# Gate's last products ahead of up's, a signal of silu's own, and an earlier turn of h in the last tiles of a mixture-of-experts layer

## The chip, the cores and the metric

The kernel runs on one core of one Trainium2 chip. The metric is the device time in microseconds. Where a time comes from a profile, it is counted from the start of the profiled span.

## What is computed

`x` has 4 x 512 tokens of 512 numbers. Each token goes through a linear layer with a low-rank adapter chosen per batch; the result `y` goes through a top-2 mixture of 16 experts, and the experts' weighted output is added to `x`. Cut to what matters here:

```python
def _L0_ffn_ref(hidden_states, gate_w, w_gate, w_up, w_down):
    ...
    g = jnp.einsum('th,eih->tei', x, w_gate)
    u = jnp.einsum('th,eih->tei', x, w_up)
    h = jax.nn.silu(g) * u
    expert_out = jnp.einsum('tei,ehi->teh', h, w_down)
    y = jnp.einsum('te,teh->th', combine, expert_out)
```

Hidden size is 512, an expert's inner size 352 (three parts of 128, 128 and 96), everything in float32.

## The kernel before

A first phase computes `y`, the router and tables that sort the 4096 token-expert pairs by expert, in **tiles** of 128 pairs of one expert. There are at least 32 tiles (`NFULL`) and at most 47 (`NTILE`); the number is found on the chip, and with these inputs it is 40, tiles 0 to 39. From tile 32 on each engine's code stands in branches on that count.

Each engine has its own program, written in order, and semaphores join them. For a tile t:

- GpSimd gathers its 128 rows of `y` into `xg`, and later scatters the result `ys` into `out`, adding.
- TensorE transposes `xg` into bank 0 (`x_turn`, L569). ScalarE rounds it to `xt_hi` (L732), VectorE takes the rest as `xt_lo` (L1067). A float32 product is made of three: hi x hi, hi x lo, lo x hi, for which the weights too are split, once per expert, into `w_hi` (ScalarE, L340) and `w_lo` (VectorE, L342) from `w_raw`.
- `gate_up` (L636): for each quarter k of the 512 inner rows six products of 352 columns, three for gate into bank 2 or 3, three for up into bank 4 or 5, the two taken in turns. After the 24th `m_gu` is raised.
- ScalarE waits for `m_gu` and makes `sg` = silu(gate) (L779). VectorE waits for `a_sg` and multiplies it by up: `hh` (L1079). TensorE transposes `hh` into bank 1 (`h_turn`, three transposes, L613), ScalarE rounds that to `ht_hi` (L769), VectorE makes `ht_lo` (L1072, raises `v_ht`).
- `down` (L657): nine products of 512 columns into bank 6 or 7, three for each of three inner parts k. ScalarE scales the bank by the token's weight: `ys` (L788).

The order on TensorE is by hand. In iteration t of the main loop, up to 32, it is h_turn(t-1), x_turn(t+1), gate_up(t), down(t-1). From tile 32 on h_turn(t) stands inside down(t-1):

```python
if t + 1 >= NFULL and t + 1 < NTILE and k == KI - 1:
    h_turn(t + 1)
```

that is, after six of the nine products. VectorE's order in an iteration from 32 on is: ht_lo of the tile before (once, at 32), the gate_up part of tile t+1's `w_lo` if its expert is new, xt_lo(t+1), hh(t), ht_lo(t), the down part of `w_lo`. ScalarE's is xt_hi(t+1), the gate_up part of `w_hi` for tile t+2, silu(t), the down part for t+1, ht_hi(t), ys(t-1); at 32, ht_hi(31) stands ahead of these.

## Time and profile before

| | us |
|---|---|
| median of 3 runs | 366.63 |
| runs | 365.82, 366.63, 366.96 |
| the profiled execution's own time | 366.1 |
| its span, first to last instruction | 364.3 |
| TensorE busy | 349.9 (96%) |
| VectorE busy | 198.1 (54%) |
| ScalarE busy | 179.3 (49%) |

The mean granted TensorE clock is 0.993 of full speed. The page names L636 and L657, gate_up and down, for 36% and 20% of the chain that ended last. TensorE's matmuls are pipelined: the time of one (0.32 us for 352 columns) overlaps the next, so the rate is read from start to start. PE is TensorE, PEld its weight loads, which run ahead of the products; DVE is VectorE, ACT ScalarE, POOL GpSimd, SP SyncE; a q behind a name means its sequencer.

### The profile page before, as it was taken

To read this page: it belongs to the slowest core of one execution; us is meant where nothing else is said; L and a number is where in the kernel's file an instruction comes from. 1 tells how busy PE (TensorE), PEld (TensorE's weight loads), DVE (VectorE), ACT (ScalarE), POOL (GpSimd) and SP (SyncE) were. 2 spreads that over 40 slices of the span, in tenths; PEclk is the share of its full clock that TensorE was granted. 3 is DMA by queue.
4 is the path that set the end of the run, shared out by engine and by line. 5 is a ranking of instruction groups with operands and counts; after the bars stand their busy time and mean duration, and the time that the engine had idled before them with its cause. 6 is when DMAs were issued, how large, how long until landed. Compare 5 with 4: busy or idle time off the path is not lost.

```text
span 364.3 us, 7564 instructions
## 1 busy us (share of the span) xinstructions
PE 349.9 (96%) x2033; PEld 310.0 (85%) x2033; DVE 198.1 (54%) x274; ACT 179.3 (49%) x242; POOL 129.4 (36%) x85
## 2 busy tenths in 40 slices
PE   8999989999999999999999999999999999999980
PEld 4777778879989999999999999999999998898960
DVE  0566799894546355444665527556282656556210
ACT  2488611622575544445755466464545557554320
POOL 0000000042534354366644526546264554232131
PEclk9999999999999999999999999999999999999997
DMA  7994763766498758669598684976929295921322
GB/s 278 398 444 144 297 231 120 271 227 221 119 346 288 223 130 226 153 146 319 111 302 252 180 280 68 299 207 186 332 44 304 62 248 176 303 33 14 48 34 36
DMA packets 28913, 73.78 MB, mean 203 GB/s; under 512 B 3440, under 2 KB 3568, under 8 KB 28784
## 3 DMA queue, kind: packets, MB, share of 16 engines
q1 hardware_dynamic: 19904, 54.30, 42.4%
q0 software_dynamic: 8960, 18.89, 24.0%
q8 instruction: 23, 0.38, 0.4%
q14 instruction: 26, 0.21, 0.2%
HBM read 60.59 MB, written 19.92 MB: 221 GB/s over the span
## 4 chain that ended last, share of the span: by engine, by line
PE 81%; DMA 6%; issue 6%; DVE 2%; ACT 1%; DVEq 1%; POOLq 1%; SPq 0%; POOL 0%; ACTq 0%
PE bank L636 36%; PE bank L657 20%; PE bank L569 4%; PE bank L613 4%; PE bank L507 4%; PE bank L508 3%; PE bank L509 3%; PE bank L404 3%; DMA xg<-y_rows,gidx 2%; DMA w_raw<-wall 2%; DMA head_sb<-head 2%; PE bank L435 1%; PE bank L555 1%; PE bank L517 1%; DVE hh L1079 1%
## 5 line engine op out<-in xcount | busy, mean ns | idle before, releaser
L1152 POOL DMA_INDIRECT out<-ys,sidx x40 | 75.4, 1886 | 131.0 <-ACT ys L788 60.5
L342 DVE TENSOR_TENSOR w_lo<-w_raw,w_hi (+2 forms) x32 | 76.4, 2389 | 22.0 <-ACT w_hi L340 16.5
L1131 POOL DMA_INDIRECT xg<-y_rows,gidx x40 | 53.4, 1335 | 97.8 <-issue 83.4
L636 PE MATMUL bank<-w_hi,xt_hi 128*128 x320 | 80.8, 333 | 0.3 <-issue 0.3
L636 PE MATMUL bank<-w_hi,xt_lo 128*128 x320 | 77.2, 322 | 0.0
L636 PE MATMUL bank<-w_lo,xt_hi 128*128 x320 | 77.2, 322 | 0.0
L340 ACT ACTIVATE w_hi<-w_raw (+2 forms) x32 | 64.8, 2024 | 10.1 <-issue 6.1
L779 ACT ACTIVATE sg<-bank 128x352 f32<-128x352 f32 x40 | 18.6, 464 | 79.0 <-PE bank L636 75.9
L636 PEld LDWEIGHTS bank<-w_hi,xt_lo 128*128 128x128 f32 x320 | 55.8, 188 | 0.0
L636 PEld LDWEIGHTS bank<-w_lo,xt_hi 128*128 128x128 f32 x320 | 55.7, 188 | 0.0
L636 PEld LDWEIGHTS bank<-w_hi,xt_hi 128*128 128x128 f32 x320 | 53.9, 189 | 1.3 <-issue 1.3
L1079 DVE TENSOR_TENSOR hh<-sg,bank 128x352 f32<-128x352 f32 x40 | 20.7, 518 | 56.1 <-ACT sg L779 56.1
L657 PE MATMUL bank<-w_hi,ht_hi 128*128 (+1 forms) x120 | 47.9, 399 | 0.9 <-ACT ys L788 0.9
L1072 DVE TENSOR_TENSOR ht_lo<-bank,ht_hi 128x384 fp32r<-128x384 f32 x40 | 22.2, 555 | 48.5 <-ACT ht_hi L769 48.5
L657 PE MATMUL bank<-w_lo,ht_hi 128*128 (+1 forms) x120 | 47.2, 394 | 0.0
L657 PE MATMUL bank<-w_hi,ht_lo 128*128 (+1 forms) x120 | 47.0, 392 | 0.0
L788 ACT ACTIVATE ys<-bank,wtab 128x512 f32<-128x512 f32 x40 | 27.3, 683 | 32.7 <-PE bank L657 31.1
L1067 DVE TENSOR_TENSOR xt_lo<-bank,xt_hi 128x512 fp32r<-128x512 f32 x40 | 27.4, 686 | 3.5 <-ACT xt_hi L732 3.5
L657 PEld LDWEIGHTS bank<-w_hi,ht_lo 128*128 128x128 f32 (+1 forms) x120 | 22.5, 188 | 5.0
L657 PEld LDWEIGHTS bank<-w_hi,ht_hi 128*128 128x128 f32 (+1 forms) x120 | 22.6, 188 | 4.4 <-issue 1.4
L507 PE MATMUL bank<-w_base_hi,x_hi 128*128 128x512 f32 x64 | 25.8, 403 | 0.3 <-DVE x_lo L863 0.3
L732 ACT ACTIVATE xt_hi<-bank 128x512 fp32r<-128x512 f32 x40 | 23.9, 598 | 4.0 <-PE bank L569 3.9
(177 smaller groups left out, 369.6 us busy)
## 6 DMA issues: line engine op xcount, KB each, us to landing
w_raw<-wall SPq DMA_DIRECT2D x16, 1408.0 KB
w_raw<-wall SPq DMA_DIRECT2D x16, 768.0 KB
x_st<-xt SPq DMA_DIRECT2D x8, 512.0 KB, 13.5
y_rows<-y_st SPq DMA_DIRECT2D x16, 256.0 KB, 4.7
head_sb<-head SPq DMA_DIRECT2D x2, 640.0 KB, 5.1
wb_sb<-wb SPq DMA_DIRECT2D x2, 512.0 KB, 9.0
wbt_sb<-wbt SPq DMA_DIRECT2D x2, 512.0 KB, 10.8
xg<-y_rows,gidx POOLq DMA_INDIRECT x40, 6.2
```

Of the source, the lines that this page charges most:

```text
L340: e.activation(hi, raw, ACT.Copy).then_inc(own, 1)
L342: e.tensor_tensor(w_lo[:, bass.ds(dst, n)], raw, hi, ALU.subtract).then_inc(own, 1)
L507: e.matmul(dst, hi, whi, start=k == 0, stop=False, skip_group_check=True)
L636: mm = e.matmul(bank[2 + 2 * s + t % 2][:, 0:INTER], a, w[:, bass.ds(at + (k * GU + s * INTER), INTER)], start=k == 0 and a is hi and w is ...
L657: mm = e.matmul(bank[6 + t % 2][:], a, w[0:n, bass.ds(at + (GUW + k * H), H)], start=k == 0 and a is hi and w is w_hi, stop=k == KI - 1 an ...
L732: e.activation(xt_hi[t % 2][:], bank[0][:], ACT.Copy).then_inc(a_xt, 1)
L788: e.activation(ys[t % NYS][:], bank[6 + t % 2][:], ACT.Copy, scale=wtab[:, t:t + 1]).then_inc(a_ys, 1)
L1067: e.tensor_tensor(xt_lo[t % 2][:], bank[0][:], xt_hi[t % 2][:], ALU.subtract).then_inc(v_xt, 1)
L1072: e.tensor_tensor(ht_lo[t % 2][:], bank[1][:, 0:KI * P], ht_hi[t % 2][:], ALU.subtract).then_inc(v_ht, 1)
L1079: e.tensor_tensor(hh[t % 2][:], sg[t % 2][:], bank[4 + t % 2][:, 0:INTER], ALU.mult).then_inc(v_h, 1)
L1131: e.indirect_dma_start(out=xg[t % NXG][:], out_offset=None, in_=y_dram, in_offset=bass.IndirectOffsetOnAxis(ap=gidx[:, t:t + 1], axis=0)). ...
L1152: e.indirect_dma_start(out=out, out_offset=bass.IndirectOffsetOnAxis(ap=sidx[:, t:t + 1], axis=0), in_=ys[t % NYS][:], in_offset=None, bou ...
```

## The change

Three things are changed. In the last quarter of gate_up (k = 3) gate's three products come ahead of up's, and the last of gate's raises a new semaphore `m_ga`. silu waits for `m_ga` instead of `m_gu`, and the product `hh` waits for `m_gu` itself, besides `a_sg`. From tile 32 on h_turn(t+1) stands in down(t) behind four products instead of six; and down waits for `v_ht` last of its waits instead of first.

```diff
--- before.py
+++ after.py
@@ -256,7 +256,7 @@
         d_s = [sem(f"d_s{i}") for i in range(NYS)]
         p_turn = sem("p_turn")
         a_gu, a_dn, v_gu, v_dn = sem("a_gu"), sem("a_dn"), sem("v_gu"), sem("v_dn")
-        m_xt, m_gu, m_ht, m_dn = sem("m_xt"), sem("m_gu"), sem("m_ht"), sem("m_dn")
+        m_xt, m_ga, m_gu, m_ht, m_dn = [sem("m_" + n) for n in ("xt", "ga", "gu", "ht", "dn")]
         a_xt, v_xt, a_sg, v_h, a_ht, v_ht, a_ys = [
             sem(n) for n in ("a_xt", "v_xt", "a_sg", "v_h", "a_ht", "v_ht", "a_ys")]
 
@@ -631,29 +631,32 @@
                         if t == 2 and k == KH // 2:
                             h_turn(t - 1)
                         hi, lo = (v[t % 2][:, k * P:(k + 1) * P] for v in (xt_hi, xt_lo))
-                        for a, w, last in ((hi, w_hi, False), (hi, w_lo, False), (lo, w_hi, True)):
-                            for s in range(2):
-                                mm = e.matmul(bank[2 + 2 * s + t % 2][:, 0:INTER], a,
-                                              w[:, bass.ds(at + (k * GU + s * INTER), INTER)],
-                                              start=k == 0 and a is hi and w is w_hi,
-                                              stop=k == KH - 1 and last)
+                        trio = ((hi, w_hi), (hi, w_lo), (lo, w_hi))
+                        pairs = [(s, i) for i in range(3) for s in range(2)]
+                        for s, i in pairs if k < KH - 1 else sorted(pairs):
+                            a, w = trio[i]
+                            mm = e.matmul(bank[2 + 2 * s + t % 2][:, 0:INTER], a,
+                                          w[:, bass.ds(at + (k * GU + s * INTER), INTER)],
+                                          start=k == 0 and i == 0, stop=k == KH - 1 and i == 2)
+                            if k == KH - 1 and (s, i) == (0, 2):
+                                mm.then_inc(m_ga, 1)
                     mm.then_inc(m_gu, 1)
 
             def down(t):
                 with in_use(e, count, t):
                     run, _, _, at = words[t]
-                    e.wait_ge(v_ht, t + 1)
                     e.wait_ge(v_dn, run + 1)
                     if t == 1:
                         e.wait_ge(v_w, 1)
                     if t >= 2:
                         e.wait_ge(a_ys, t - 1)
+                    e.wait_ge(v_ht, t + 1)
                     for k in range(KI):
-                        if t + 1 >= NFULL and t + 1 < NTILE and k == KI - 1:
-                            h_turn(t + 1)
                         n = P if k < KI - 1 else ILAST
                         hi, lo = (v[t % 2][0:n, k * P:(k + 1) * P] for v in (ht_hi, ht_lo))
                         for a, w, last in ((hi, w_hi, False), (hi, w_lo, False), (lo, w_hi, True)):
+                            if NFULL <= t + 1 < NTILE and k == 1 and w is w_lo:
+                                h_turn(t + 1)
                             mm = e.matmul(bank[6 + t % 2][:], a, w[0:n, bass.ds(at + (GUW + k * H), H)],
                                           start=k == 0 and a is hi and w is w_hi, stop=k == KI - 1 and last)
                     mm.then_inc(m_dn, 1)
@@ -770,7 +773,7 @@
 
             def silu(t):
                 with in_use(e, count, t):
-                    e.wait_ge(m_gu, t + 1)
+                    e.wait_ge(m_ga, t + 1)
                     if t == 0:
                         for i in range(NYST):
                             e.wait_ge(d_y[i], 16 * (CH // NYST))
@@ -1074,6 +1077,7 @@
             def product(t):
                 with in_use(e, count, t):
                     e.wait_ge(a_sg, t + 1)
+                    e.wait_ge(m_gu, t + 1)
                     if t >= 2:
                         e.wait_ge(m_ht, t - 1)
                     e.tensor_tensor(hh[t % 2][:], sg[t % 2][:], bank[4 + t % 2][:, 0:INTER], ALU.mult).then_inc(v_h, 1)
```

TensorE, the last six products of the last gate_up in the program (bank2 is gate's, bank4 up's). Before:

```order
L636 ISA
L636 MATMUL bank2<-w_hi_49,xt_hi0_122 128x352
L636 ISA
L636 MATMUL bank4<-w_hi_49,xt_hi0_122 128x352
L636 REGISTER_ALU
L636 MATMUL bank2<-w_lo_50,xt_hi0_122 128x352
L636 REGISTER_ALU
L636 MATMUL bank4<-w_lo_50,xt_hi0_122 128x352
L636 MATMUL bank2<-w_hi_49,xt_lo0_124 128x352
L636 MATMUL bank4<-w_hi_49,xt_lo0_124 128x352
```

Now:

```order
L638 ISA
L638 MATMUL bank2<-w_hi_49,xt_hi0_122 128x352
L638 REGISTER_ALU
L638 MATMUL bank2<-w_lo_50,xt_hi0_122 128x352
L638 MATMUL bank2<-w_hi_49,xt_lo0_124 128x352
L638 ISA
L638 MATMUL bank4<-w_hi_49,xt_hi0_122 128x352
L638 REGISTER_ALU
L638 MATMUL bank4<-w_lo_50,xt_hi0_122 128x352
L638 MATMUL bank4<-w_hi_49,xt_lo0_124 128x352
```

Gate's bank is finished three products ahead of up's; the number of products and of register operations is the same.

TensorE, the last down that holds a turn (L613, the transposes of h). Before:

```order
L657 MATMUL bank7<-w_hi_49,ht_hi1_127 128x512
L657 REGISTER_ALU
L657 MATMUL bank7<-w_lo_50,ht_hi1_127 128x512
L657 MATMUL bank7<-w_hi_49,ht_lo1_129 128x512
L271 COMPARE_AND_BRANCH
L613 MATMUL bank1<-cs_144,hh0_120 128x128 [waits v_ht,v_h]
L613 MATMUL bank1<-cs_144,hh0_120 128x128
L613 MATMUL bank1<-cs_144,hh0_120 96x128
L271 UNCONDITIONAL_BRANCH
L657 ISA
L657 MATMUL bank7<-w_hi_49,ht_hi1_127 128x512
L657 REGISTER_ALU
```

Now:

```order
L660 MATMUL bank7<-w_hi_49,ht_hi1_127 128x512
L271 COMPARE_AND_BRANCH
L613 MATMUL bank1<-cs_144,hh0_120 128x128 [waits v_ht,v_h]
L613 MATMUL bank1<-cs_144,hh0_120 128x128
L613 MATMUL bank1<-cs_144,hh0_120 96x128
L271 UNCONDITIONAL_BRANCH
L660 REGISTER_ALU
L660 MATMUL bank7<-w_lo_50,ht_hi1_127 128x512
L660 MATMUL bank7<-w_hi_49,ht_lo1_129 128x512
L660 ISA
L660 MATMUL bank7<-w_hi_49,ht_hi1_127 128x512
```

The turn and the branches around it stand behind the first product of the second inner part; five products follow it where three did.

TensorE, the head of the last down of the program. Before:

```order
L279 COMPARE_AND_BRANCH
L646 REGISTER_ALU [waits v_ht]
L646 REGISTER_ALU
L657 ISA [waits a_ys,v_dn]
L657 MATMUL bank6<-w_hi_49,ht_hi0_126 128x512
L657 REGISTER_ALU
```

Now:

```order
L279 COMPARE_AND_BRANCH
L648 REGISTER_ALU x2
L660 ISA [waits v_ht,a_ys,v_dn]
L660 MATMUL bank6<-w_hi_49,ht_hi0_126 128x512
L660 REGISTER_ALU
```

The wait for v_ht has moved from the first register operation to the instruction behind both. On VectorE nothing changes place; the row of `hh` carries [waits m_ht,m_gu,a_sg] where it carried [waits m_ht,a_sg], and on ScalarE that of `sg` waits for m_ga in m_gu's place.

## Rows read from the trace of the kernel before

**Rows 1.** The page: the span, and TensorE's busy time.

```profile
span 364.3 us, 7564 instructions
...
PE 349.9 (96%) x2033; PEld 310.0 (85%) x2033; DVE 198.1 (54%) x274; ACT 179.3 (49%) x242; POOL 129.4 (36%) x85
```

**Rows 2.** Busy time by stretch: full tiles, then tiles 32 to 39.

```profile
110.20:297.10 186.90, 186.90 (x1122) 174.94 (x1121) 98.97 (x106) 99.70 (x134) 94.77 (x58) 1.00 0.72 205
297.10:352.40 55.30, 54.03 (x316) 48.66 (x314) 27.89 (x30) 26.40 (x38) 16.95 (x10) 1.00 0.49 118
```

**Rows 3.** The chain that ended last: start, us, what; full tiles.

```profile
284.05 3.88 PE bank L636 x24
287.93 2.07 PE bank L657 x9
...
290.76 3.81 PE bank L636 x24
```

**Rows 4.** Waits of PEld, 296 to 353: us in total, times, longest.

```profile
PEld bank L613 <- DVE hh L1079: 2.2, 7, 0.6
```

**Rows 5.** Timeline around turn 32: start, us, engine, line, what.

```profile
297.78 0.56 DVE L1072 TENSOR_TENSOR ht_lo<-bank,ht_hi 128x384 fp32r<-128x384 f32 x1 [2.16 <-ACT ht_hi L769]
...
298.62 3.09 DVE L342 TENSOR_TENSOR w_lo<-w_raw,w_hi  x1 [0.28 <-issue]
...
301.12 0.40 PE L657 MATMUL bank<-w_hi,ht_hi 128*128 x1
...
301.32 0.47 ACT L779 ACTIVATE sg<-bank 128x352 f32<-128x352 f32 x1 [3.08 <-PE bank L636]
...
301.63 0.68 DVE L1067 TENSOR_TENSOR xt_lo<-bank,xt_hi 128x512 fp32r<-128x512 f32 x1
...
302.23 0.51 DVE L1079 TENSOR_TENSOR hh<-sg,bank 128x352 f32<-128x352 f32 x1
...
302.80 0.55 PE L613 MATMUL bank<-cs,hh 128*128 128x128 f32 x3
```

**Rows 6.** Timeline around turn 33.

```profile
304.07 0.69 ACT L788 ACTIVATE ys<-bank,wtab 128x512 f32<-128x512 f32 x1
...
305.52 2.56 ACT L340 ACTIVATE w_hi<-w_raw  x1 [0.28 <-issue]
...
308.11 0.39 PE L657 MATMUL bank<-w_hi,ht_hi 128*128 x1
...
308.31 0.46 ACT L779 ACTIVATE sg<-bank 128x352 f32<-128x352 f32 x1 [0.23 <-PE bank L636]
...
308.81 0.52 DVE L1079 TENSOR_TENSOR hh<-sg,bank 128x352 f32<-128x352 f32 x1 [1.05 <-ACT sg L779]
...
309.38 0.34 PEld L613 LDWEIGHTS bank<-cs,hh 128*128 128x128 f32 x3 [0.16 <-DVE hh L1079]
309.49 0.49 PE L613 MATMUL bank<-cs,hh 128*128 128x128 f32 x3
```

**Rows 7.** Timeline around turns 34 and 36.

```profile
310.54 0.56 DVE L1072 TENSOR_TENSOR ht_lo<-bank,ht_hi 128x384 fp32r<-128x384 f32 x1 [1.21 <-ACT ht_hi L769]
...
316.49 0.55 PE L613 MATMUL bank<-cs,hh 128*128 128x128 f32 x3
...
330.26 0.29 PEld L613 LDWEIGHTS bank<-cs,hh 128*128 128x128 f32 x3 [0.50 <-DVE hh L1079]
```

**Rows 8.** Start of the last down; first row: sequencer instructions of L646, times.

```profile
L646 PEldq ALU_OP  x2: 36/36/36, 351.9 to 352.0; - x2
...
351.08 0.39 PE L657 MATMUL bank<-w_hi,ht_lo 96*128 x1
351.34 0.56 DVE L1072 TENSOR_TENSOR ht_lo<-bank,ht_hi 128x384 fp32r<-128x384 f32 x1 [1.22 <-ACT ht_hi L769]
...
352.39 0.19 PEld L657 LDWEIGHTS bank<-w_hi,ht_hi 128*128 128x128 f32 x1 [1.35 <-issue]
352.40 0.49 PE L657 MATMUL bank<-w_hi,ht_hi 128*128 x1 [0.92 <-ACT ys L788]
```

## The prediction

> **What bounds the kernel now.** I read the page's busy lines first, then busy time by stretch, then the chain that ended last, then TensorE's waits, and last the timeline of single tiles. The busy lines [rows 1] give TensorE 349.9 us of a span of 364.3 us. By stretch [rows 2], TensorE is busy for the whole of 110.20 to 297.10 us at a granted clock of 1.00 (its faster level, 2.4 GHz), that is, tiles 4 to 31 leave it no gap; from 297.10 to 352.40 us it is busy 54.03 of 55.30 us, so 1.3 us is all that is open there. The chain [rows 3] shows full tiles: 24 gate_up products in 3.81 or 3.88 us, 0.160 us each on average, and nine down products in 2.07 us, 0.230 us each, one behind the other. In that stretch silu, the product on VectorE and the evacuations lie beside TensorE, so an earlier silu buys nothing. What can change is where TensorE waits for h: from tile 32 on, where h_turn(t), three transposes that I call turn t, stands inside down(t-1).
>
> TensorE's waits for hh in the tail [rows 4] are 2.2 us over seven turns, counted in the weight loads. The load stands ahead of its product, so not all of this is lost by the products. The timeline shows two kinds of turn.
>
> *Turns with a backlog on VectorE* [rows 5]: down(31) begins at 301.12; six products end at 301.12 + 6 x 0.23 = 302.50; turn 32 begins at 302.80. TensorE stands 0.30. silu began at 301.32, soon after gate_up, but hh began only at 302.23, because VectorE was on w_lo (3.09 us, from 298.62) and then xt_lo (0.68, from 301.63). Turns 34 and 36 look the same [rows 7].
>
> *Turns without a backlog* [rows 6]: down(32) begins at 308.11, silu at 308.31 (0.20 after), hh at 308.81 (0.70 after), its 0.52 end at 309.33, the weight load of turn 33 starts at 309.38 and the transposes at 309.49, which is 308.11 + 6 x 0.23. TensorE loses nothing. Turns 35, 37, 38 and 39 have this pattern too: of the 2.2 us [rows 4], turns 32, 34 and 36 hold 0.56, 0.56 and 0.50, and the rest is short waits of the load alone.
>
> *The end* [rows 8]: the last product of down(38) starts at 351.08 and its slot ends at 351.31. down(39) starts at 352.40: it needs ht_lo(39), which runs 351.34 to 351.90. TensorE stands 1.09 us.
>
> **The change, part by part.** I count how much later each event comes than before, in the profiled execution.
>
> *Order of the last six gate_up products.* Six products with six weight loads before, six and six after. Cost 0 on count. What is new is that neighbours now add into one PSUM bank, four times per tile. Down's nine all do so and take 0.23 us for 512 columns, where 512 / 2.4 GHz is 0.213; gate_up's alternate and take 0.160 for 352, where 0.147 is streaming [rows 3]. The excess is 17 ns against 13.5 ns. Were all of the difference the bank's, 4 x 3.5 ns x 40 tiles = 0.6 us would come on top; I take 0, as it fits the longer product as well, and keep 0.6 as upper bound. The lower bound is 0. Nothing here can shorten a product.
>
> The Trainium skill, page "TensorE: Matmul & The Clock Gate", section "Back-to-back issue gap", gives N / 2.4 + 2.5 ns for a warm matmul. That would be 149 and 216 ns. Its form has no term for the bank, so by it this part costs 0 too.
>
> *silu on its own signal.* It now starts when gate's last product is done, three products or 3 x 0.16 = 0.48 us earlier: 0.28 before down begins rather than 0.20 after. It takes 0.46, so it is done 0.18 after. The product hh waits in addition for up (m_gu), seen 0.20 after, as silu saw it before. So hh can begin at +0.20 plus whatever a further wait costs, instead of +0.70. No row shows a wait on two such signals on VectorE. The nearest is the step from silu's start to hh's, 0.50 with silu's own 0.46 in it [rows 6], which leaves 0.04 for a signal; I take 0.08 for the two, so hh at +0.28 and done at +0.80. Bounds: +0.20 and +0.70 (no gain at all). Queued behind hh on VectorE are ht_lo and the next w_lo. They need hh's own result first, so the added wait delays nothing else.
>
> The Trainium skill, page "Advanced Engine Details and Errata", section "Network/Comms", gives 50 to 100 ns for a sequencer's reading of a semaphore. By that, hh begins at +0.25 to +0.30, and the margin that I work out next shrinks or holds, but is not used up. No row here shows it on VectorE.
>
> *Turn two products earlier.* It is now due 4 x 0.23 = 0.92 after down begins, not 1.38.
> - Turns 33, 35, 37, 38, 39: hh done at +0.80, the load 0.05 later at +0.85, due at +0.92. No wait. Bounds: 0, and 0.46 each if hh is no earlier. At turn 33 ScalarE is in the way: its w_hi split (2.56 us from 305.52, behind ys(31) at 304.07, which waits for the end of down(31)) moves 0.46 later with TensorE and ends at 308.54. silu(33), due at 308.57 - 0.28 = 308.29, starts at about 308.50 and hh 0.50 later at 309.00, 0.15 behind the pattern's 308.85. That is 0.08 more than the margin: **+0.08 us**, with bounds 0 and 0.15.
> - Turn 32: hh hangs on VectorE's w_lo and xt_lo. These follow ht_lo(31) at 297.78 [rows 5], whose turn is at the head of the iteration and isn't moved. So the turn starts at 302.80 as before, the wait grows from 0.30 to 0.76, and five instead of three products are still to come. **+0.46 us** for all that follows. Bounds: 0 (if VectorE came free earlier) and 0.46.
> - Turns 34 and 36: hh(34) hangs on a rigid row of VectorE work that begins with ht_lo(33) at 310.54, and thus on turn 33. From turn 33 at 309.49 to turn 34 at 316.49 are 7.00 us [rows 6, 7]. TensorE has the same work between the two turns as before, since both moved by two products. Same distance, same wait: **0**. Bounds 0 on both sides.
>
> *The end.* Turn 39 comes at +0.46 + 0.08 - 0.46 = 0.08 later than before in absolute time, ht_lo(39) ends at 351.98; down(38)'s five remaining products end at 351.31 + 0.54 = 351.85, now ahead of it. So the start of down(39) hangs on ht_lo(39) as before. From ht_lo(39)'s end at 351.90 to the first weight load at 352.39 there is 0.49: the wait on v_ht sits on the first of two register operations [rows 8], then come a wait and a further operation. The change puts v_ht last in the source and the compiled order carries it on the wait behind the two register operations. Two steps of four go, about 0.19 of 0.49. Bounds 0 and 0.49. Start of down(39): 352.40 + 0.08 - 0.19 = 352.29. **Net -0.11 us.** All behind it, nine products, ys and the last scatter, is unmoved in length.
>
> *Tiles 0 to 31.* Only silu's and hh's starts move. Their cover is TensorE's unbroken work [rows 2]; without it the gain would be 0.48 per tile. A moved v_ht wait is met before TensorE's sequencer gets there: 0.
>
> **Sum** against the profiled execution (366.1 us, of which the span is 364.3 and 1.8 lies around it): turns +0.54, taken up again at the end by the idle time there (1.09 becomes 0.44), net -0.1. That is 366.0. The median of the runs shown is 366.63, 0.5 above this execution, so I forecast **366.5 us**. The expected gain of an earlier h lies almost wholly in a gap that turn 32 fills with its own longer wait.
>
> **The rivals.**
> 1. *hh isn't earlier, and the early turns wait (slower).* If the signal of gate's last product or the third wait on VectorE costs what silu's lead gives, hh stays at +0.70 and each of the turns 33, 35, 37, 38 and 39 stands up to 0.46 and passes it on: the start of down(39) comes 5 x 0.46 - 0.19 = 2.1 us later, 368.7 by the median. It decides from 0.24 us per turn on (5 x 0.24 - 0.1 = 1.1 us). For it: the margin is only 0.07. Against it: signals take 0.04 [rows 6]. Small misses of 0.05 would give +0.25 in all, 366.8.
> 2. *Turn 32 doesn't hold (faster).* If VectorE were free earlier there, the turns cost 0.08 only and down(39) starts about 0.6 earlier than before: 366.0. Against it: nothing that feeds the w_lo split ahead of it is moved.
> 3. *Same-bank neighbours cost.* +0.6 us, 367.1. Against it: down's rate.
> 4. *The change does not do what it says*, the scheduler undoing it. The compiled order shows the moves as written, so this has no share.
>
> **How the numbers follow.** About 0.3% (1.1 us) is what a measurement of this kernel can tell from no change. Forecast 0.78, rival 1 at its full size 0.06, rival 2 0.08, rival 3 0.08. Only rival 1, with something of rival 3 on top of small misses, is slower by over 0.3%: 0.07. Faster by over 0.3% needs -1.1 us, more than the lower bounds give together (0.46 at turn 32 and 0.49 at the end are 0.95), so only what I have not seen: 0.04. Same: 0.89. The runs of before alone spread from 365.8 to 367.0, so the range has half of that around rivals 2 and 3: 365.6 to 367.4.
>
> **What would show it.** Right: turn 32 at four products with a wait near 0.76; turns 34 and 36 with the waits of before; 33, 35, 37, 38, 39 with their transposes 0.92 after down's start; silu 0.28 before down's first product; TensorE's standing time before the last down down from 1.09 to about 0.4, with the down(39) load about 0.3 behind ht_lo's end; a tile of the full stretch unchanged. Wrong: hh later than +0.35 in turns 37 to 39, turn 32 earlier than 302.8, or a full tile longer than before by more than 0.01 us.

## The result, and the profile after

The changed kernel takes 367.38 us (median of 22 runs, 366.62 to 369.00), the kernel before 366.45 (22 runs between them, 365.40 to 368.44). The ratio is 1.0032 with an interval of 1.0020 to 1.0044: slower by 0.9 us, where 0.1 us faster was forecast. The median lies at the upper edge of the forecast's range (365.6 to 367.4). The profiled execution of the changed kernel has a span of 365.5 us, 1.2 more than that of before.

The page of the changed kernel: its span, and its busy lines.

```profile
span 365.5 us, 7566 instructions
...
PE 351.9 (96%) x2033; PEld 311.4 (85%) x2033; DVE 197.7 (54%) x274; ACT 180.0 (49%) x242; POOL 136.3 (37%) x85
```

Against [rows 1] TensorE is busy 2.0 us longer, with as many products. The span grew by less, so idle time went as well. I read the two apart.

The chain that ended last, changed kernel, full tiles: start, us, what.

```profile
264.70 0.33 PE bank L613 x3
...
265.47 3.88 PE bank L638 x24
269.34 2.09 PE bank L660 x9
...
272.20 3.87 PE bank L638 x24
...
278.16 0.33 PE bank L613 x3
```

In [rows 3] the tiles alternate: 24 products in 3.81 us, then in 3.88, and down's nine in 2.07. Now each tile has the long form: 3.88, 3.87, and down's nine, whose order nobody touched, take 2.09. In the chain turn, x_turn, gate_up and down follow one another without a gap, so this is no wait. Two tiles, from one turn to the next but one, take 278.16 - 264.70 = 13.46 us. For before the same view gives:

```profile
263.29 0.33 PE bank L613 x3
...
276.64 0.33 PE bank L613 x3
```

That is 13.35 us, with gate_up in 3.81 and 3.88. The difference, 0.11 us per two tiles, is there from tile 5 to tile 31, thirteen times: 1.4 us.

The tail, tile 32 first. Timeline of the changed kernel.

```profile
299.49 0.56 DVE L1075 TENSOR_TENSOR ht_lo<-bank,ht_hi 128x384 fp32r<-128x384 f32 x1 [2.61 <-ACT ht_hi L772]
...
302.54 0.46 ACT L782 ACTIVATE sg<-bank 128x352 f32<-128x352 f32 x1 [2.59 <-PE bank L638]
...
302.83 0.39 PE L660 MATMUL bank<-w_hi,ht_hi 128*128 x1
...
303.94 0.51 DVE L1083 TENSOR_TENSOR hh<-sg,bank 128x352 f32<-128x352 f32 x1
...
304.50 0.55 PE L613 MATMUL bank<-cs,hh 128*128 128x128 f32 x3 [0.59 <-DVE hh L1083]
```

It answers to [rows 5]. VectorE's chain ht_lo, w_lo, xt_lo, hh stands as before in its distances: from ht_lo to hh 4.45 us, there and here. silu has moved ahead of down (302.54 against 302.83), hh has not. Four products end at 302.83 + 0.92 = 303.75, the turn starts at 304.50: TensorE stands 0.75 us, where it stood 0.30.

Timeline of the changed kernel, turn 33.

```profile
307.70 2.56 ACT L340 ACTIVATE w_hi<-w_raw  x1 [0.28 <-issue]
...
310.16 0.45 ACT L782 ACTIVATE sg<-bank 128x352 f32<-128x352 f32 x1
...
310.36 0.39 PE L660 MATMUL bank<-w_hi,ht_hi 128*128 x1
...
310.64 0.52 DVE L1083 TENSOR_TENSOR hh<-sg,bank 128x352 f32<-128x352 f32 x1 [1.78 <-ACT sg L782]
...
311.29 0.49 PE L613 MATMUL bank<-cs,hh 128*128 128x128 f32 x3
```

Against [rows 6]: hh begins 0.28 after down and not 0.70; w_hi on ScalarE holds silu up until 310.16, 0.20 ahead of down, and hh follows silu's end (310.61) by 0.03. The transposes start 0.93 behind down all the same, when their four products are through: this turn doesn't wait.

Timeline of the changed kernel, end of down(38) and start of down(39).

```profile
350.51 0.47 ACT L782 ACTIVATE sg<-bank 128x352 f32<-128x352 f32 x1 [2.71 <-PE bank L638]
...
350.80 0.39 PE L660 MATMUL bank<-w_hi,ht_hi 128*128 x1
...
351.06 0.52 DVE L1083 TENSOR_TENSOR hh<-sg,bank 128x352 f32<-128x352 f32 x1 [4.04 <-ACT sg L782]
...
351.73 0.49 PE L613 MATMUL bank<-cs,hh 128*128 128x128 f32 x3
...
352.78 0.56 DVE L1075 TENSOR_TENSOR ht_lo<-bank,ht_hi 128x384 fp32r<-128x384 f32 x1 [1.20 <-ACT ht_hi L772]
353.00 0.40 PE L660 MATMUL bank<-w_hi,ht_lo 96*128 x1
...
353.64 0.19 PEld L660 LDWEIGHTS bank<-w_hi,ht_hi 128*128 128x128 f32 x1 [0.68 <-issue]
```

Against [rows 8]: silu begins 0.29 ahead of down, hh 0.26 behind its start, the transposes 0.93 behind it. The last product of down(38) has its slot until 353.23, ht_lo(39) ends at 353.34, the load is at 353.64, 0.30 behind it, where it was 0.49. TensorE stands 0.42 us instead of 1.09.

The balance of the two profiled executions, each stretch from the timeline (turn t is the start of its transposes):

| stretch | before | after | difference |
|---|---|---|---|
| start of the span to turn 5 | 122.89 | 123.21 | +0.32 |
| turn 5 to turn 31 | 173.59 | 174.98 | +1.39 |
| turn 31 to first product of down(39) | 55.92 | 55.46 | -0.46 |
| from there to the end of the span | 11.89 | 11.88 | -0.01 |

The sum is +1.24. The first stretch isn't the change's: in the sixteen kernels below turn 5 starts anywhere from 122.38 to 124.18, with no order in it by edit. It is why spans of single executions are not compared here, but stretches.

### The profile page after: what moved, and what is told of

It reads as the page before. It is cut to its first block, busy times and chain, and to the rows that moved or that the text cites. A ratio compares the mean times of both kernels' runs of the same rounds, so it can differ in the third digit from the quotient of the medians.

```text
span 365.5 us, 7566 instructions
## 1 busy us (share of the span) xinstructions
PE 351.9 (96%) x2033; PEld 311.4 (85%) x2033; DVE 197.7 (54%) x274; ACT 180.0 (49%) x242; POOL 136.3 (37%) x85
## 4 chain that ended last, share of the span: by engine, by line
PE 93%; DMA 2%; issue 1%; DVE 1%; POOLq 1%; ACT 0%; POOL 0%; DVEq 0%
PE bank L638 43%; PE bank L660 23%; PE bank L569 5%; PE bank L404 4%; PE bank L613 4%; PE bank L507 4%; PE bank L508 3%; PE bank L509 3%; DMA xg<-y_rows,gidx 2%; PE bank L420 1%; PE bank L435 1%; PE bank L555 1%; PE bank L517 1%; POOLq L92 0%; PE bank L490 0%
## 5 line engine op out<-in xcount | busy, mean ns | idle before, releaser
L1156 POOL DMA_INDIRECT out<-ys,sidx x40 | 77.5, 1938 | 124.5 <-ACT ys L791 69.8
L1135 POOL DMA_INDIRECT xg<-y_rows,gidx x40 | 58.3, 1457 | 98.5 <-issue 83.6
L638 PE MATMUL bank<-w_hi,xt_hi 128*128 x320 | 87.6, 334 | 0.3 <-issue 0.3
L638 PE MATMUL bank<-w_hi,xt_lo 128*128 x320 | 84.1, 324 | 0.0
L638 PE MATMUL bank<-w_lo,xt_hi 128*128 x320 | 83.8, 323 | 0.0
L638 PEld LDWEIGHTS bank<-w_lo,xt_hi 128*128 128x128 f32 x320 | 56.9, 189 | 0.0
L638 PEld LDWEIGHTS bank<-w_hi,xt_lo 128*128 128x128 f32 x320 | 56.9, 188 | 0.0
L638 PEld LDWEIGHTS bank<-w_hi,xt_hi 128*128 128x128 f32 x320 | 55.2, 190 | 1.0 <-issue 0.9
L660 PE MATMUL bank<-w_lo,ht_hi 128*128 (+1 forms) x120 | 48.1, 401 | 0.0
L660 PE MATMUL bank<-w_hi,ht_hi 128*128 (+1 forms) x120 | 47.1, 393 | 0.3 <-DVE ht_lo L1075 0.3
```

The source lines that it names most:

```text
L638: mm = e.matmul(bank[2 + 2 * s + t % 2][:, 0:INTER], a, w[:, bass.ds(at + (k * GU + s * INTER), INTER)], start=k == 0 and i == 0, stop=k = ...
L660: mm = e.matmul(bank[6 + t % 2][:], a, w[0:n, bass.ds(at + (GUW + k * H), H)], start=k == 0 and a is hi and w is w_hi, stop=k == KI - 1 an ...
L1135: e.indirect_dma_start(out=xg[t % NXG][:], out_offset=None, in_=y_dram, in_offset=bass.IndirectOffsetOnAxis(ap=gidx[:, t:t + 1], axis=0)). ...
L1156: e.indirect_dma_start(out=out, out_offset=bass.IndirectOffsetOnAxis(ap=sidx[:, t:t + 1], axis=0), in_=ys[t % NYS][:], in_offset=None, bou ...
```

## The experiments

Each kernel computes all that the reference asks. The table gives for each the median beside that of the kernel before on the same chip, the ratio with its interval, and two stretches of its profile. The ratio is not the quotient of the two medians, and where they differ (e10) I go by the ratio. Most kernels have 9 to 12 runs; e7 has 6 and e13 only 4. "Two tiles" is from turn 5 to turn 31 divided by 13, "tail" from turn 31 to the first product of down(39). For before they are 13.35 and 55.92, for the changed kernel 13.46 and 55.46. The tails of the kernels that edit the order alone lie at 55.78 to 55.94, but for e8's 55.64, where gate_up runs at another pace in these tiles too: a difference of 0.15 in a tail says nothing by itself, and smaller ones are read from single turns.

| kernel | us, before beside it | ratio (interval) | two tiles | tail |
|---|---|---|---|---|
| e1 order only | 368.26, 366.42 | 1.0044 (1.0025 to 1.0063) | 13.46 | 55.79 |
| e2 signal only | 366.85, 366.42 | 1.0023 (0.9999 to 1.0046) | 13.36 | 55.69 |
| e3 tail only | 368.77, 366.42 | 1.0062 (1.0041 to 1.0084) | 13.35 | 57.78 |
| e4 all, from tile 32 on | 365.98, 366.42 | 0.9982 (0.9965 to 0.9998) | 13.35 | 55.46 |
| e5 bank pairs | 366.31, 366.33 | 1.0008 (0.9993 to 1.0023) | 13.35 | 55.82 |
| e6 more switches | 365.89, 366.33 | 0.9993 (0.9978 to 1.0009) | 13.35 | 55.78 |
| e7 lo first | 367.69, 366.33 | 1.0044 (1.0024 to 1.0064) | 13.46 | 55.91 |
| e8 all quarters | 366.67, 366.33 | 1.0000 (0.9974 to 1.0026) | 13.35 | 55.64 |
| e9 e4, turn 32 at six | 365.69, 366.66 | 0.9981 (0.9965 to 0.9997) | 13.35 | 55.00 |
| e10 e4, v_ht first | 366.07, 366.66 | 1.0000 (0.9972 to 1.0027) | 13.35 | 55.70 |
| e11 e4, all turns at six | 366.13, 366.66 | 0.9989 (0.9972 to 1.0007) | 13.35 | 55.39 |
| e12 change, all quarters | 366.43, 366.66 | 0.9987 (0.9963 to 1.0011) | 13.35 | 55.32 |
| e13 first quarter only | 368.77, 366.50 | 1.0066 (1.0044 to 1.0089) | 13.45 | 55.90 |
| e14 last two quarters | 366.92, 366.50 | 1.0009 (0.9988 to 1.0030) | 13.35 | 55.94 |
| e15 last three quarters | 368.16, 366.50 | 1.0036 (1.0017 to 1.0056) | 13.45 | 55.80 |
| e16 up first | 366.96, 366.50 | 1.0008 (0.9993 to 1.0024) | 13.37 | 55.84 |

### Which part of the change costs

The profile says that the full tiles are longer, not which edit makes them so: the order, the signal on a product, the third wait on VectorE and the tail's branches came together. The first four kernels take them apart. In what follows `pairs` is the list of (projection, part) that gate_up walks through, projection 0 being gate, 1 up, and part 0, 1, 2 being hi x w_hi, hi x w_lo, lo x w_hi.

**e1**, the order alone (the 3.96 and 3.89 us of its expectation run from gate_up's first product to down's first; in the chain the same groups have 3.88 and 3.81):

```diff
-                        for a, w, last in ((hi, w_hi, False), (hi, w_lo, False), (lo, w_hi, True)):
-                            for s in range(2):
+                        pairs = [(s, i) for i in range(3) for s in range(2)]
+                        for s, i in sorted(pairs) if k == KH - 1 else pairs:
```

> The kernel before with the one edit that in the last quarter of gate_up gate's three products come ahead of up's; silu still waits for m_gu, the turn stands behind six products, the v_ht wait is first. In the trace of the change two neighbouring full tiles take 13.46 us against 13.35 of before, from tile 4 to 31 some 1.5 us. Order theory (the order of the six products sets TensorE's pace): two full tiles at 13.46, the 24 products at 3.96 us in every tile instead of 3.89 and 3.96 in turn, time +1.5 us, about 368.0 beside 366.5. Signal theory (the earlier silu beside up's last products, or the extra signal, slows TensorE): two full tiles at 13.35, time within 0.3 us of before.

**e2**, the signal alone, in the order of before, where gate's last product is the fifth of six:

```diff
+                            if k == KH - 1 and (s, i) == (0, 2):
+                                mm.then_inc(m_ga, 1)
...
-                    e.wait_ge(m_gu, t + 1)
+                    e.wait_ge(m_ga, t + 1)
...
+                    e.wait_ge(m_gu, t + 1)
```

> The kernel before with its order of products, but gate's last product, now the last but one, raises m_ga, silu waits for m_ga (one product, 0.16 us, earlier than before), and the product hh waits for m_gu as well; turn and v_ht wait as before. Order theory: two full tiles at 13.35 us, time within 0.3 us of before, turns 33, 35, 37 to 39 without wait. Signal theory: two full tiles at 13.40 to 13.46, time +0.7 to +1.5 us.

**e3**, the turn at four products and v_ht last, silu still on m_gu:

```diff
-                    e.wait_ge(v_ht, t + 1)
...
+                    e.wait_ge(v_ht, t + 1)
...
-                        if t + 1 >= NFULL and t + 1 < NTILE and k == KI - 1:
-                            h_turn(t + 1)
...
+                            if NFULL <= t + 1 < NTILE and k == 1 and w is w_lo:
+                                h_turn(t + 1)
```

> The kernel before with the turn behind four products and v_ht awaited last, but gate and up in turns and silu on m_gu. This is the rival of the prediction in which hh isn't earlier: turns 33, 35, 37, 38, 39 stand 0.46 us each, turn 32 as in the change 0.75. Order theory and signal theory: full tiles as before (13.35 for two), tail 2.1 us longer, time +2.1, about 368.6. If any edit of TensorE's program shifts the pace of the full tiles (placement theory), two full tiles differ from 13.35 here too.

**e4**, all edits of the change, but from tile 32 on alone (v_ht comes last in every tile, as in the change; silu waits for m_gu up to tile 31 and for m_ga from 32 on, and hh waits for m_gu from 32 on):

```diff
+                        for s, i in sorted(pairs) if k == KH - 1 and t >= NFULL else pairs:
...
+                            if k == KH - 1 and (s, i) == (0, 2) and t >= NFULL:
+                                mm.then_inc(m_ga, 1)
```

> The change with the new order, the signal m_ga and the wait on it only from tile 32 on; tiles 0 to 31 as before. Order theory and signal theory: two full tiles at 13.35 us and the tail of the change, which is 0.46 us shorter than that of before from turn 31 to the start of the last down: time -0.4 to -0.5, about 366.0. Placement theory: full tiles may lie at 13.46, and the time is then that of the change, 367.4.

The chain in e1, full tiles: two turns that lie two tiles apart.

```profile
265.32 0.33 PE bank L613 x3
...
278.78 0.33 PE bank L613 x3
```

The same view of e2.

```profile
263.34 0.33 PE bank L613 x3
...
276.69 0.33 PE bank L613 x3
```

e1 has 278.78 - 265.32 = 13.46, e2 276.69 - 263.34 = 13.35 (13.36 over all thirteen pairs). So the order alone does all of it, and the signal and the third wait do none; in e2 silu begins only one product earlier, so the much earlier silu is cleared by e1, which pays without it. (e2's ratio by itself, 1.0023 with a bound at 0.9999, would leave this open.) e4 keeps the old order up to tile 31 and has 13.35; its tail has the 55.46 of the changed kernel, and its median is below before's. That is the change without its cost.

e3 has the condition of rival 1: the early turns without an earlier h. Waits of PEld in the tail of e3: us in total, times, longest.

```profile
PEld bank L613 <- DVE hh L1079: 5.3, 8, 1.0
```

The same of the changed kernel.

```profile
PEld bank L613 <- DVE hh L1083: 2.9, 8, 1.0
```

The loads of the turns wait 5.3 us in e3 and 2.9 in the changed kernel, and the tail is 57.78 - 55.92 = 1.86 us longer than before's. I had worked out 2.1 for that rival, from 0.46 for each of five turns. In e3's timeline each turn from 33 to 39, 34 and 36 among them, starts 1.27 behind down where 0.92 was due: it stands 0.35, not 0.46.

### What it is in the order

With order as the cause there were two readings: what lies next to what in a bank (rival 3), or the sequence of operands. Three orders of the last quarter, and gate first in all four.

**e5**: g0 g1 u0 u1 g2 u2, two same-bank neighbours instead of four.

```diff
+                        for s, i in [(0, 0), (0, 1), (1, 0), (1, 1), (0, 2), (1, 2)] if k == KH - 1 else pairs:
```

> The kernel before, but in the last quarter gate and up follow as gate, gate, up, up, gate, up: twice two neighbours add into one bank, the stationary operands stay xt_hi four times, then xt_lo twice. Bank theory (neighbours in one bank slow TensorE): two full tiles at 13.40 to 13.46 us, time +0.7 to +1.5. Operand theory (more changes between xt_hi and xt_lo slow it): 13.35, time within 0.3 us of before.

**e6**: g0 u2 g1 u0 g2 u1, no same-bank neighbours, but the operands in another sequence.

```diff
+                        for s, i in [(0, 0), (1, 2), (0, 1), (1, 0), (0, 2), (1, 1)] if k == KH - 1 else pairs:
```

> The kernel before, but the last quarter's six products stand as gate hi, up lo, gate hi, up hi, gate lo, up hi (hi, lo: the rows' part that is the stationary operand): the banks alternate as before, the stationary operand changes as often as in the change. Bank theory: two full tiles at 13.35 us, time within 0.3 us of before. Operand theory: 13.46, time +1.5.

**e7**: g2 g0 g1 u0 u1 u2, the banks as in the change, the operands in another sequence.

```diff
+                        for s, i in [(0, 2), (0, 0), (0, 1), (1, 0), (1, 1), (1, 2)] if k == KH - 1 else pairs:
```

> The kernel before, but gate's three products ahead of up's with gate's xt_lo product first: neighbours in one bank as in the change (four times), changes of the stationary operand as in before. Bank theory: two full tiles at 13.46 us, time +1.5. Operand theory: 13.35, time within 0.3 us of before.

**e8**: gate first in all four quarters, sixteen same-bank neighbours in a tile.

```diff
+                        for s, i in sorted(pairs):
```

> The kernel before with gate's three products ahead of up's in all four quarters of gate_up. If each such six costs by itself (0.106 us over two tiles for one quarter each), four quarters cost 0.42: two full tiles at 13.78 us, time +6. If the order only decides which of two paces TensorE falls into (products 0.158 or 0.161 us apart), two full tiles stay at 13.46 or return to 13.35, time +1.5 or 0.

The operands are not it: within the six products the stationary operand changes once in before, three times in the change, four times in e6 and twice in e7 (the counts in the expectations of e6 and e7 are off by one). e6 has the most and 13.35, e7 fewer than the change and its 13.46. A price per same-bank neighbour is not it either: e5 has two and pays nothing, and e8 has four times the change's and pays nothing. The chain of e8, full tiles:

```profile
264.10 0.33 PE bank L613 x3
...
264.87 3.84 PE bank L638 x24
268.71 2.07 PE bank L658 x9
...
271.55 3.82 PE bank L638 x24
275.37 2.09 PE bank L658 x9
277.45 0.33 PE bank L613 x3
```

Two tiles take 277.45 - 264.10 = 13.35, but not as before takes them: gate_up has 3.84 and 3.82, and down's nine alternate between 2.07 and 2.09. So one order can run at more than one pace. In before a short and a long gate_up alternate from tile to tile, in e1 every tile has the long one. Buffers and banks alternate from tile to tile too (`t % 2`); whether they are what the alternation hangs on, no run tries.

Where the time is lost shows in the starts of the products. Timeline of PE in before, one full tile of the short kind, first products of its second and fourth quarter:

```profile
264.85 0.48 PE L636 MATMUL bank<-w_hi,xt_hi 128*128 x2
...
266.75 0.48 PE L636 MATMUL bank<-w_hi,xt_hi 128*128 x2
```

The same of the changed kernel, the tile in the same place.

```profile
266.27 0.48 PE L638 MATMUL bank<-w_hi,xt_hi 128*128 x2
...
268.21 0.33 PE L638 MATMUL bank<-w_hi,xt_hi 128*128 x1
```

The second and third quarter take 0.95 each in before and 0.97 in the changed kernel, and nobody touched their order. On average over tiles 6 to 29, every second tile of before takes 6.642 us and now 6.734, the others took 6.711 and now take 6.726. The reordered quarter itself is at most 0.003 longer than one of the long kind. The change thus pays hardly anything in its own six products; it puts the other quarters of every second tile, and down's nine in each, on a longer spacing. In before the products of the short kind start 0.156 and 0.160 apart by turns, those of the long kind 0.158, 0.159, 0.164 and 0.165.

### The tail: what the turns and the wait are worth

**e9**, e4 with turn 32 alone put back behind six products, to test the one term of the tail that was a loss:

```diff
-                            if NFULL <= t + 1 < NTILE and k == 1 and w is w_lo:
+                            if (t + 1 == NFULL and k == 2 and a is hi and w is w_hi) or (
+                                    NFULL < t + 1 < NTILE and k == 1 and w is w_lo):
```

> e4 (all edits from tile 32 on only) with turn 32 alone left behind six products, where VectorE's backlog holds it anyway. By the sums of the prediction the wait at turn 32 falls from 0.75 to 0.30 us and all behind it comes 0.46 earlier: from turn 31 to the first product of the last down 55.0 us, where e4 and the change have 55.46 and before 55.92; time 0.4 below e4, about 365.5 to 365.6, 0.9 below before. If something else holds the tail (the sequencer, ScalarE), it stays at 55.4 and the time at 366.0.

**e10**, e4 with `e.wait_ge(v_ht, t + 1)` first in down's waits, as before:

```diff
+                    e.wait_ge(v_ht, t + 1)
                     e.wait_ge(v_dn, run + 1)
...
-                    e.wait_ge(v_ht, t + 1)
```

> e4 with the wait for v_ht first again in down. By the prediction two sequencer steps of four come back behind ht_lo(39): from turn 31 to the last down's first product 55.65 us instead of 55.46, from the end of ht_lo(39) to that product 0.50 instead of 0.31, time +0.2 on e4. If the place of the wait is worth nothing: 55.46 and 0.31.

**e11**, e4 with all turns behind six products:

```diff
-                            if NFULL <= t + 1 < NTILE and k == 1 and w is w_lo:
+                            if NFULL <= t + 1 < NTILE and k == 2 and a is hi and w is w_hi:
```

> e4 with all turns behind six products. What is left of the change in the tail is the place of the v_ht wait, and an early silu without use: from turn 31 to the last down's first product 55.73 us (before 55.92, less 0.19), turn 32 waits 0.30, time about 0.2 to 0.3 over e4. If the early turns were worth nothing by themselves: 55.46.

**e12**, the change with `sorted(pairs)` in all four quarters, as in e8:

```diff
-                        for s, i in pairs if k < KH - 1 else sorted(pairs):
+                        for s, i in sorted(pairs):
```

> The change as it is, with gate's three products ahead of up's in all four quarters instead of the last alone. If only TensorE's pace made the change slow, two full tiles return from 13.46 to 13.353 us with every other edit in place, the tail stays at 55.46, and the time is that of e4, about 366.0, 1.4 below the change. If the signal or the waits take part in the pace, two full tiles stay at 13.46 and the time at 367.4.

e9's tail is 55.00, 0.46 less than e4's: that is turn 32's term to the hundredth. It has the shortest tail and the lowest median of the study, with a ratio of 0.9981 (0.9965 to 0.9997) to before. It is faster than before; the intervals don't tell it from e4, and it didn't run beside the changed kernel, whose ratio to before is 1.0032.

For e10, the timeline of ht_lo(39) and of the first load of down(39), in e4:

```profile
351.21 0.56 DVE L1078 TENSOR_TENSOR ht_lo<-bank,ht_hi 128x384 fp32r<-128x384 f32 x1 [1.19 <-ACT ht_hi L772]
...
352.07 0.19 PEld L660 LDWEIGHTS bank<-w_hi,ht_hi 128*128 128x128 f32 x1 [0.70 <-issue]
```

The same in e10.

```profile
352.41 0.56 DVE L1078 TENSOR_TENSOR ht_lo<-bank,ht_hi 128x384 fp32r<-128x384 f32 x1 [1.20 <-ACT ht_hi L772]
...
353.46 0.19 PEld L660 LDWEIGHTS bank<-w_hi,ht_hi 128*128 128x128 f32 x1 [0.88 <-issue]
```

From ht_lo's end to the load: 352.07 - 351.77 = 0.30 with v_ht last, 353.46 - 352.97 = 0.49 with v_ht first. The tails of e4 and e10 differ by 0.24. The place of a wait among its neighbours in the source is worth 0.19 of that, where the wait is the one that comes last.

e11's tail is 55.39 where I expected 55.73. The early turns of the change are thus worth nothing (55.46 against 55.39), as long as turn 32 is among them; without it they are worth 0.39 (e9 against e11). The expectation called the early silu of no use with late turns, and that was wrong: from turn 38 to turn 39 e11 takes 6.26 us and e2 6.33, where before takes 6.49. The signal alone takes away a stand there, which is looked at in the next part. e12 shows that the pace is had back in the changed kernel too: 13.35. Its ratio to before, 0.9987 (0.9963 to 1.0011), doesn't tell it from before.

### How many quarters

e1 has gate first in one quarter and pays, e8 in four and doesn't. e13 does it in the first quarter alone, e14 in the last two, e15 in the last three; e16 puts up first in the last quarter.

```diff
e13:
+                        for s, i in sorted(pairs) if k == 0 else pairs:
e14:
+                        for s, i in sorted(pairs) if k >= KH - 2 else pairs:
e15:
+                        for s, i in sorted(pairs) if k >= 1 else pairs:
e16:
+                        for s, i in [(1 - s, i) for s, i in sorted(pairs)] if k == KH - 1 else pairs:
```

> The kernel before with gate's three products ahead of up's in the first quarter alone. If the pace is lost because a single quarter differs from the rest, wherever it is: two full tiles 13.46 us, time +1.5. If it is the place, next to down, that counts: 13.353, time within 0.3 us of before.

> The kernel before with gate's three ahead of up's in the last two quarters. Place theory (last quarter next to down): 13.46 us for two full tiles, against which e8, all quarters, speaks. Number theory (each such quarter shifts TensorE's phase and the sum decides): any of 13.353, 13.46 or a third value; no number is favoured.

> The kernel before with gate's three ahead of up's in the last three quarters. Same theories as for e14: place theory 13.46, number theory any of the values; both know e8 (four quarters) at 13.353 and e1 (one) at 13.46.

> The kernel before with up's three products ahead of gate's in the last quarter. If only the pattern three in one bank, three in the other counts, 13.46 us for two full tiles as with gate first; if it matters that silu's bank is closed early or late, 13.353.

The chain of e13, turns two tiles apart:

```profile
264.37 0.33 PE bank L613 x3
...
277.82 0.33 PE bank L613 x3
```

The same view of e14, which has gate_up in 3.82 and 3.85 by turns (e13 has 3.87 throughout).

```profile
263.89 0.33 PE bank L613 x3
...
264.65 3.82 PE bank L638 x24
...
277.24 0.33 PE bank L613 x3
```

e13 takes 13.45 and e14 13.35. It is not the place: the first quarter costs what the last one does. Over before and the kernels that differ from it in how many quarters put gate's three first (e1, e8, e13, e14, e15), an even number of such quarters (none, two, four) gives 13.35 and an odd one (one, three) 13.45 to 13.46. That describes these six kernels and is not shown as a rule: two quarters were tried in one arrangement and three in one, and e5 and e6, which reorder one quarter in other ways, pay nothing. e16 is nearly free (13.37), though its number is one. It isn't a mirror of e1 either: the quarter ahead ends on up, so up's bank takes four products in a row. Two tiles come to the same 13.353 us in before, e5, e6, e8 and e14, though they spread it differently over their quarters. Why TensorE has these paces, and what passes them on from one quarter or tile to the next, stays open.

## Why the prediction was wrong, point by point

- **Order of the last six gate_up products: wrong, and this decides the result.** The step was "I take 0" and, for tiles 0 to 31, that only silu's and hh's starts move. Measured: +0.107 us per two tiles (e1 against before, 1.39 / 13 in the balance), 1.4 us in all and more than twice the upper bound of 0.6. The runs show what stood in the place of that 0: the order of one quarter sets the spacing of the products in the other quarters and tiles. The bound failed in its form. It multiplied an excess per neighbour by the number of neighbours, and e5 and e8 show that the cost doesn't go by neighbours; and it averaged gate_up's two values of 3.81 and 3.88 in [rows 3] to 0.160 a product, though they alternate from tile to tile without exception. Why TensorE behaves so stays open. Rival 3 named the right place and the wrong law. Its chance of 0.08 was low for a part of the kernel in which each 1% of pace is 1.9 us of the 186.9 in [rows 2].
- The sentence from the Trainium skill, page "TensorE: Matmul & The Clock Gate", section "Back-to-back issue gap", spoke for 0 as well: its 149 ns for 352 columns holds nothing of an order. The section gives that formula for a single matmul by itself, not for a stream with weight loads, which this is. The runs differ from it. 3.81 us over 24 products is 159 ns, 3.88 is 162, and which of the two it is hangs on the order. The measurement decides.
- **silu and hh: right.** Taken: silu 0.28 ahead of down, hh 0.28 behind its start. Measured: 0.29 and 0.26 at turn 39. (Turn 33's 0.28 is no test of it: hh came 0.03 behind silu's end there.) ScalarE saw gate_up's last result 0.20 behind down's start [rows 6], and VectorE starts 0.06 later than that; the two engines' own shares in the 0.06 weren't separated. The page "Advanced Engine Details and Errata" of the Trainium skill, section "Network/Comms", gives 50 to 100 ns for a sequencer's reading of a semaphore. The 0.06 lies in that, but no run here measures such a reading by itself.
- **Turn 32: right.** Taken +0.46 and a wait of 0.76; measured 0.75, and e9 gives the 0.46 back. **Turn 33: the right number, by luck.** +0.08 taken; its distance from turn 32 was 6.69 [rows 5, 6] and is 311.29 - 304.50 = 6.79. But the taken cause, ScalarE holding silu up so that the turn waits, did not act: the transposes start 0.93 behind down, as at turns 37 to 39. The gate_up between turns 32 and 33 takes 3.96 us from its first product to down's first, where before takes 3.89. That is again the spacing of the products, and the kernels that edit the order alone and leave the turns where they were have 6.74 to 6.80 here too.
- **Turns 35, 37, 38, 39: right.** Their transposes start 0.92 to 0.93 behind down, without a wait. **Turns 34 and 36**: taken 0. Measured against turn 33 and turn 35, turn 34 came 0.08 and turn 36 0.05 earlier, which is what the w_lo split of the two tiles took less (3.17 and 3.14 us before, 3.09 and 3.09 now). The split has values from 3.09 (e1) to 3.16 (e14) in kernels that don't touch the tail too, so this is not the change's.
- **The end: right in its kind.** Taken: stands 0.44, the load about 0.3 behind ht_lo. Measured: 0.42 and 0.30, with e10 as the other side of the comparison.
- **The tail's net: the right sign, too small.** Taken -0.11, measured -0.46. Of the 0.35 between them, 0.13 is the two splits, and 0.18 lies between turns 38 and 39, 6.49 us before and 6.31 now; the rest is spread over the other turns. Before had a stand there that I had not looked at. Timeline of before, end of down(37) and start of gate_up(39):

```profile
344.59 0.39 PE L657 MATMUL bank<-w_hi,ht_lo 96*128 x1
...
344.90 0.32 PEld L636 LDWEIGHTS bank<-w_hi,xt_hi 128*128 128x128 f32 x2 [0.35 <-issue]
344.91 0.59 PE L636 MATMUL bank<-w_hi,xt_hi 128*128 x2
...
345.34 0.32 PE L636 MATMUL bank<-w_lo,xt_hi 128*128 x1
```

  The same place in e2, which has the signal but the turn behind six products:

```profile
344.57 0.40 PE L660 MATMUL bank<-w_hi,ht_lo 96*128 x1
344.80 0.54 PE L638 MATMUL bank<-w_hi,xt_hi 128*128 x2
345.18 0.32 PE L638 MATMUL bank<-w_lo,xt_hi 128*128 x1
```

  The last of the three products behind the turn starts at 344.59, with its slot to 344.82, and the next product at 344.91: 0.09 lost, the load being held up by nothing but its own sequencer ("issue"). The second product of the pair comes late as well: from down's last to the third product are 345.34 - 344.59 = 0.75 us in before and 347.25 - 346.69 = 0.56 in the changed kernel, and this 0.19 is all of the 0.18. In the changed kernel five products follow the turn, and hh is earlier. Either is enough to take nearly all of it away. e3 has the five without an earlier hh, and takes 0.55 over the same products. e2 and e11 have the earlier hh and still three products, and take 0.61 and 0.55. In e2 and e11 the turn's first load starts 0.23 us ahead of its transposes, in before 0.13. That the sequencer thereby comes free earlier and gets through its branches in time is my reading of it.
- **The rivals.** Rival 1 did not come, by its own condition: hh is at +0.26 to +0.28, and the margin held. Its price was tried by e3, 1.86 us in the tail for 2.1 taken, with 0.35 and not 0.46 at each turn. Rival 2 did not come. The change did what it says, which was not enough: it is the tail's 0.46 against the full tiles' 1.39.
- **What was named as a sign** showed it at once: "a full tile longer than before by more than 0.01 us". It is 0.05.

## What to carry to other kernels

Where one engine is busy without a gap for half of the kernel, an edit of the order of its instructions needs a price per instruction in every pass of the loop, even where the count stays; an edit that pays in the last eight tiles is best confined to these, as e4 shows. Two durations of one and the same group that alternate strictly are not scatter, and a change of order can put all of it on the worse side. Among waits of one place, the one whose event comes last belongs last (0.19 us in e10), and a turn that is late already gains nothing from being asked for earlier: it puts work behind the wait that could have stood ahead of it (0.46 us, given back in e9).

## What the runs showed of the hardware that was not expected

- The order in which products alternate between two PSUM banks moved the pace of TensorE by 0.8%: 13.35 or 13.46 us for the 80 products of two tiles (and their 80 loads), with the same operands and count and at a granted clock of 1.00 in both, as [rows 2] show for before and the next rows for the changed kernel (busy time by stretch, full tiles; behind the time and the busy columns stands PEclk).

```profile
110.20:297.10 186.90, 186.90 (x1114) 174.71 (x1113) 98.74 (x106) 100.33 (x134) 96.96 (x58) 1.00 0.71 205
```

- The pace carries over to products whose order was never changed: down's nine, in other banks, take 2.07 or 2.09 us, and the second and third quarter of gate_up 0.95 or 0.97 each.
- With gate's three products in a row in none, two or four quarters two tiles take 13.35 us, with one or three 13.45 to 13.46, and with up first in one quarter 13.37. Whether odd and even is the rule behind it is not shown.
